# Linear attention: the last sum of a tile moved from VectorE to a ScalarE copy and a GpSimd sum

## The chip, the core and the metric

The kernel runs on one core of a Trainium2 chip. The metric is the device time of one execution in microseconds (us). The engines are TensorE (PE, with its weight loads as PEld), VectorE (DVE), ScalarE (ACT), GpSimd (POOL) and SyncE (SP). Each works through its own queue in order, and the order between engines is made by waits on semaphores.

## What is computed

The input x has 2048 rows of 128 floats. Four blocks follow each other, each on the layer norm of x and added back to x: softmax attention (16 heads of 64), a mixture of experts (8 experts, one chosen per row), a linear attention (16 heads of 8), and the same mixture of experts again. The change is in the linear attention:

```python
qkv = x @ w_qkv.T + b_qkv
q, k, v = jnp.split(qkv, 3, axis=-1)        # 16 heads of 8
q_prime = elu(q) + 1.0
k_prime = elu(k) + 1.0
kv_cumsum = cumsum(einsum('bhtd,bhte->bhtde', k_prime, v), axis=2)
context = einsum('bhtd,bhtde->bhte', q_prime, kv_cumsum)
norm = einsum('bhtd,bhtd->bht', q_prime, cumsum(k_prime, axis=2))
out = context / (norm[..., None] + EPS)
return out @ w_out.T + b_out                # added to x
```

## The kernel before

The four blocks are `attention`, `ffn`, `linear_attention` and `ffn`, with a barrier of all engines behind each. `linear_attention` (L1318) handles 16 tiles of 128 rows. Every engine runs the same software pipeline, `in_turn` (L1374): turn n emits, for each stage with offset off, the work on tile n - off, in the order in which the stages stand in that engine's dictionary. The offsets and that order are written out by hand, engine by engine; there is no planner. Buffers come in pairs (tile t uses number t % 2), and waits on counters keep a buffer from being overwritten.

The path of tile t:

- norm, GpSimd, turn t (L1393): xn is x less its mean, times 1/deviation, with statistics from VectorE made ahead of the pipeline.
- xT, turn t: TensorE transposes (L1575), ScalarE copies to SBUF (L1492).
- z, turn t + 1: TensorE projects to q, k, v (L1581); ScalarE makes neg, v and ex (L1504 to L1507). features on VectorE (L1446) make qk of them.
- turn t + 2: TensorE transposes q (L1548, copied by ScalarE at L1482), GpSimd makes outer, the products of k and v with 1152 columns (L1413), TensorE adds to past (L1554, L1556; ScalarE copies it, L1487), then makes the prefix sums within the tile as a matmul of outer with a triangle (L1564), and inter, the part of earlier tiles (L1571). VectorE multiplies the sums with q (prod, L1439).
- heads, VectorE, turn t + 3: reduce (L1449), add inter (L1453), den (L1457, L1459), and o (L1463). GpSimd masks past into state (L1402), read by inter of tile t + 1.
- turn t + 4: TensorE transposes o (L1585), ScalarE copies it (oT, L1512). GpSimd adds the output bias into x (bias, L1397).
- y, turn t + 5: TensorE projects oT into `out` in PSUM (L1544), one bank, not a pair; VectorE adds `out` to x (L1435). TensorE's y of the next tile waits for that sum (s_x).

The orders, with offsets: GpSimd norm 0, outer 2, state 3, bias 4. VectorE heads 3, features 1, y 5, sums 2. ScalarE qT 2, z 1, xT 0, past 2, oT 4. TensorE qT 2, z 1, y 5, xT 0, sums 2, oT 4. The second and third transposes share a PSUM bank with the first, so TensorE's qT of a turn waits for ScalarE's oT copy of the turn before (L1525). The last tile's work ends in turn 20.

Of the kernel before, what the change touches and what calls it, by code (L numbers as in the profile page):

```python
# [10 lines left out]
ALU = mybir.AluOpType  # L11
ACT = mybir.ActivationFunctionType
AX = mybir.AxisListType

P = 128
# [1302 lines left out]
def linear_attention(nc, shp, keep):  # L1318

    D, NT = shp.D, shp.NT  # L1320
# [3 lines left out]
    U = 2  # L1324
    x, ident = keep["x"], keep["ident"]
# [4 lines left out]
    with ExitStack() as ctx:  # L1330
        def sb(name, shape, dt=F32):
            return ctx.enter_context(nc.sbuf_tensor("li_" + name, shape, dt))

        def pair(name, shape):
            return [sb(f"{name}{k}", shape) for k in range(U)]
# [3 lines left out]
        def sem(name):  # L1339
            sems.append(nc.alloc_semaphore("li_" + name))  # L1340
            return sems[-1]

        def psum(name, cols):
# [5 lines left out]
        past, inter, out = past_ps[:, 0:VX], inter_ps[:, 0:VX], out_ps[:, 0:D]  # L1349
# [3 lines left out]
        xn, xT = pair("xn", [P, D]), pair("xT", [D, P])  # L1353
        neg, ex = pair("neg", [P, 2 * D]), pair("ex", [P, 2 * D])
        qk, v1 = pair("qk", [P, 2 * D]), pair("v1", [P, HL, DL + 1])

        outer, prod = pair("outer", [P, HL, DL + 1, DL]), sb("prod", [P, HL, DL + 1, DL])
        qT, mine, state = pair("qT", [D, P]), pair("mine", [P, VX]), pair("state", [P, VX])
        own, tot = sb("own", [P, HL, DL + 1]), sb("tot", [P, HL, DL + 1])
        den, o, oT = sb("den", [P, HL]), pair("o", [P, HL, DL]), pair("oT", [P, P])  # L1360

        s_one, s_xb, s_den = sem("s_one"), sem("s_xb"), sem("s_den")
# [1 line left out]
        s_xn, s_xTp, s_xT, s_z, s_neg, s_ex, s_v, s_qk = (sem(n) for n in ("s_xn", "s_xTp", "s_xT", "s_z", "s_neg", "s_ex", "s_v", "s_qk"))  # L1364
        s_outer, s_sums, s_prod, s_past, s_mine, s_state, s_inter = (
            sem(n) for n in ("s_outer", "s_sums", "s_prod", "s_past", "s_mine", "s_state", "s_inter"))
        s_qTp, s_qT, s_own, s_tot, s_rden, s_o, s_oTp, s_oT, s_out, s_x = (
            sem(n) for n in ("s_qTp", "s_qT", "s_own", "s_tot", "s_rden", "s_o", "s_oTp", "s_oT", "s_out", "s_x"))

        def rows_of(c):  # L1370

            return slice(0, TPC) if c == 0 else slice(TPC, NT)

        def in_turn(offsets, emit):  # L1374
            for n in range(NT + max(offsets.values())):
                for stage, off in offsets.items():
                    if 0 <= n - off < NT:
                        emit(stage, n - off, (n - off) % U)

        with nc.Block() as block:  # L1380

            @block.gpsimd
            def _(pool):
                for k in range(U):
                    pool.memset(v1[k][:, :, DL:DL + 1], 1.0).then_inc(s_one, 1)
                pool.wait_ge(li["s_bo"], 16)

                def emit(stage, t, k):
                    if stage == "norm":
                        pool.wait_ge(s_rstd, 1 if t < TPC else 2)  # L1390
                        if t >= U:
                            pool.wait_ge(s_xTp, t - U + 1)
                        pool.tensor_scalar(xn[k][:, :], x[:, t, :], mv[:, t, 0:1], rstd[:, t:t + 1],  # L1393
                                           ALU.subtract, ALU.mult).then_inc(s_xn, 1)
                    elif stage == "bias":
                        pool.wait_ge(s_xn, t + 1)
                        pool.tensor_tensor(x[:, t, :], x[:, t, :], b_out_all[:, :], ALU.add).then_inc(s_xb, 1)  # L1397
                    elif stage == "state":
                        pool.wait_ge(s_mine, t + 1)
                        if t >= U:  # L1400
                            pool.wait_ge(s_inter, t - 1)
                        pool.tensor_tensor(state[k][:, :], mine[k][:, :], block_mask[:, :, :].rearrange("p h e -> p (h e)"),  # L1402
                                           ALU.mult).then_inc(s_state, 1)
                    else:
                        pool.wait_ge(s_qk, t + 1)
                        pool.wait_ge(s_v, t + 1)
                        if t == 0:
                            pool.wait_ge(s_one, U)
                        if t >= U:
                            pool.wait_ge(s_sums, t - U + 1)  # L1410
                        kk = qk[k][:, D:2 * D].rearrange("p (h d) -> p h d", d=DL).unsqueeze(2).to_broadcast([P, HL, DL + 1, DL])
                        vv = v1[k][:, :, :].unsqueeze(3).to_broadcast([P, HL, DL + 1, DL])
                        pool.tensor_tensor(outer[k][:, :, :, :], kk, vv, ALU.mult).then_inc(s_outer, 1)  # L1413

                in_turn({"norm": 0, "outer": 2, "state": 3, "bias": 4}, emit)

            @block.vector
            def _(dve):
                for c in range(2):
                    tiles = range(NT)[rows_of(c)]  # L1420
                    for t in tiles:
                        if t % TPC == 0:
                            dve.wait_ge(keep["s_x"][t // TPC], 16)
                        dve.bn_stats(stats[:, t, :], x[:, t, :]).then_inc(s_stat, 1)
                    for t in tiles:
                        dve.wait_ge(s_stat, t + 1)
                        dve.bn_aggr(mv[:, t, :], stats[:, t, :]).then_inc(s_aggr, 1)
                    dve.wait_ge(s_std, c + 1)
                    dve.reciprocal(rstd[:, rows_of(c)], rstd[:, rows_of(c)]).then_inc(s_rstd, 1)

                def emit(stage, t, k):
                    if stage == "y":
                        dve.wait_ge(s_out, t + 1)
                        dve.wait_ge(s_xb, t + 1)
                        dve.tensor_tensor(x[:, t, :], out, x[:, t, :], ALU.add).then_inc(s_x, 1)  # L1435
                    elif stage == "sums":
                        dve.wait_ge(s_sums, t + 1)
                        qq = qk[k][:, 0:D].rearrange("p (h d) -> p h d", d=DL).unsqueeze(2).to_broadcast([P, HL, DL + 1, DL])
                        dve.tensor_tensor(prod[:, :, :, :], sums_ps[:, 0:OUTER].rearrange("p (h e d) -> p h e d", e=DL + 1, d=DL),  # L1439
                                          qq, ALU.mult).then_inc(s_prod, 1)  # L1440
                    elif stage == "features":
                        dve.wait_ge(s_ex, t + 1)
                        if t >= U:
                            dve.wait_ge(s_qTp, t - U + 1)
                            dve.wait_ge(s_past, t - U + 1)
                        dve.scalar_tensor_tensor(qk[k][:, :], z_ps[:, 0:2 * D], 0.0, ex[k][:, :], ALU.max, ALU.add).then_inc(s_qk, 1)  # L1446
                    else:
                        dve.wait_ge(s_prod, t + 1)
                        dve.tensor_reduce(own[:, :, :], prod[:, :, :, :], AX.X, ALU.add).then_inc(s_own, 1)  # L1449
                        dve.wait_ge(s_own, t + 1)  # L1450
                        if t:
                            dve.wait_ge(s_inter, t)
                            dve.tensor_tensor(tot[:, :, :], inter.rearrange("p (h e) -> p h e", e=DL + 1), own[:, :, :], ALU.add).then_inc(s_tot, 1)  # L1453
                        else:
                            dve.tensor_copy(tot[:, :, :], own[:, :, :]).then_inc(s_tot, 1)
                        dve.wait_ge(s_tot, t + 1)
                        dve.tensor_scalar(den[:, :].unsqueeze(2), tot[:, :, DL:DL + 1], EPS, None, ALU.add).then_inc(s_den, 1)  # L1457
                        dve.wait_ge(s_den, t + 1)
                        dve.reciprocal(den[:, :], den[:, :]).then_inc(s_rden, 1)  # L1459
                        dve.wait_ge(s_rden, t + 1)  # L1460
                        if t >= U:
                            dve.wait_ge(s_oTp, t - U + 1)
                        dve.tensor_tensor(o[k][:, :, :], tot[:, :, 0:DL], den[:, :].unsqueeze(2).to_broadcast([P, HL, DL]), ALU.mult).then_inc(s_o, 1)  # L1463

                in_turn({"heads": 3, "features": 1, "y": 5, "sums": 2}, emit)

            @block.scalar
            def _(act):
# [6 lines left out]
                deviation(0)  # L1475

                def emit(stage, t, k):
                    if stage == "qT":
                        act.wait_ge(s_qTp, t + 1)
                        if t > U:  # L1480
                            act.wait_ge(s_inter, t - U)
# [29 lines left out]
                            act.wait_ge(s_out, t - U + 1)  # L1511
                        act.activation(oT[k][:, :], oT_ps, ACT.Copy).then_inc(s_oT, 1)  # L1512

                in_turn({"qT": 2, "z": 1, "xT": 0, "past": 2, "oT": 4}, emit)

            @block.tensor
            def _(pe):
# [21 lines left out]
                def emit(stage, t, k):  # L1539
                    if stage == "y":  # L1540
                        pe.wait_ge(s_oT, t + 1)
                        if t:
                            pe.wait_ge(s_x, t)
                        pe.matmul(out, oT[k][:, :], wT[:, 3, :], start=True, stop=True).then_inc(s_out, 1)  # L1544
                    elif stage == "qT":
                        pe.wait_ge(s_qk, t + 1)
# [169 lines left out]
```

## Time and profile before

| what | us |
|---|---|
| median of 3 runs | 1243.08 (1242.02 to 1244.05) |
| the profiled execution, its own time | 1235.74 |
| its span | 1234.0 |
| busy: TensorE, VectorE, GpSimd, ScalarE | 1135.5, 930.9, 832.8, 808.1 |
| linear attention in the trace | about 1056 to 1141 |
| its steady part, turns 5 to 15 | 1078 to 1124 |

The trace gives the start and duration of each instruction from the start of the span. In square brackets stands how long the engine had been idle before it, and what it waited for last. `PE L1564 x6` is six matmuls merged into one row. "issue" is idle time with no wait that the profile shows. Ends of matmuls are modelled, and spans on GpSimd are rough.

### The profile page before, as it was taken

What the parts mean: (1) busy time and instruction counts of PE and PEld (TensorE: products, weight loads), DVE (VectorE), ACT (ScalarE), POOL (GpSimd) and SP (SyncE); (2) the same over time, 40 slices, a digit from 0 to 9 for tenths busy, and PEclk for the clock granted to TensorE, in tenths of its full rate; (3) what the DMA queues carried; (4) which work ended last, traced back from release to release, by engine and by line L of the source; (5) the groups of instructions that cost most, each with busy time, mean ns of one, the idle gap of its engine ahead of it and who ended that gap; (6) DMA issues with size and microseconds to landing.
All of it is one profiled execution on the core that took longest, in us unless ns stands there. A gap on an engine that the chain in (4) does not pass through costs nothing. (4 is left out here: it accounts for less than half of the span.)

```text
span 1234.0 us, 24704 instructions
## 1 busy us (share of the span) xinstructions
PE 1135.5 (92%) x8010; PEld 847.9 (69%) x8010; DVE 930.9 (75%) x2054; ACT 808.1 (65%) x2248; POOL 832.8 (67%) x814
## 2 busy tenths in 40 slices
PE   6999999999999999999999999999999669687477
PEld 4776677677767776777677767767776559354377
DVE  5887878787787778778877787788787546598645
ACT  6877676767786767777777767776777346342355
POOL 3687678857786788677677757785878435585434
PEclk9999999999999999999999999999999879799579
DMA  5000810081018002700450063002004232100131
GB/s 145 27 1 1 210 49 2 6 229 35 1 35 224 2 1 58 209 1 2 117 141 1 2 176 92 1 18 52 2 1 126 86 92 67 35 1 1 56 98 50
DMA packets 72908, 75.71 MB, mean 61 GB/s; under 512 B 8487, under 2 KB 61869, under 8 KB 72784
## 3 DMA queue, kind: packets, MB, share of 16 engines
q1 hardware_dynamic: 69776, 67.80, 20.6%
q0 software_dynamic: 3008, 6.34, 1.5%
q8 instruction: 68, 1.11, 0.4%
q14 instruction: 56, 0.46, 0.1%
HBM read 15.34 MB, written 42.91 MB: 47 GB/s over the span
## 5 line engine op out<-in xcount | busy, mean ns | idle before, releaser
L604 DVE TENSOR_REDUCE at_nmax<-at_ps 128x1 f32<-128x512 f32 (+3 forms) x640 | 374.6, 603 | 122.0 <-PE at_ps L853 119.1
L510 POOL TENSOR_SCALAR at_prob<-at_prob,at_scale 128x512 f32<-128x512 f32 (+3 forms) x307 | 424.5, 1401 | 2.0
L850 PE MATMUL at_ps<-at_k_st,at_q_parts 128*128 128x512 f32 (+3 forms) x640 | 285.6, 446 | 4.0 <-DVE at_q_parts L663 2.0
L721 ACT ACTIVATE at_prob<-at_ps,at_nmax 128x512 f32<-128x512 f32 (+3 forms) x416 | 259.9, 631 | 43.5 <-DVE at_nmax L604 42.7
L879 PE MATMUL at_ps<-at_probT,at_v 128*64 128x256 f32 (+1 forms) x2304 | 270.1, 374 | 0.6 <-DVE at_probT L627 0.6
L734 ACT ACTIVATE at_probT<-at_ps 128x512 f32<-128x512 f32 (+1 forms) x288 | 165.2, 574 | 148.8 <-PE at_ps L864 122.6
L853 PE MATMUL at_ps<-at_k_st,at_q_parts 128*128 128x512 f32 (+3 forms) x640 | 252.2, 394 | 0.0
L627 DVE COPY at_probT<-at_ps 128x512 f32<-128x512 f32 (+1 forms) x288 | 189.1, 657 | 51.6 <-PE at_ps L864 42.8
L510 POOL TENSOR_SCALAR late<-late,at_scale 128x512 f32<-128x512 f32 (+1 forms) x168 | 226.4, 1364 | 1.6
L864 PE MATMUL at_ps<-ident,at_prob 128*128 128x128 f32 x1440 | 220.1, 273 | 5.1 <-DVE at_probT L627 4.3
L879 PEld LDWEIGHTS at_ps<-at_probT,at_v 128*64 128x64 f32 x2304 | 152.1, 136 | 102.5 <-issue 40.9
L864 PEld LDWEIGHTS at_ps<-ident,at_prob 128*128 128x128 f32 x1440 | 172.8, 140 | 57.4 <-issue 23.7
L721 ACT ACTIVATE late<-at_ps,at_nmax 128x512 f32<-128x512 f32 (+1 forms) x224 | 135.4, 611 | 29.9 <-DVE at_nmax L604 27.2
L850 PEld LDWEIGHTS at_ps<-at_k_st,at_q_parts 128*128 128x128 f32 x640 | 121.0, 189 | 47.3 <-issue 27.9
L853 PEld LDWEIGHTS at_ps<-at_k_st,at_q_parts 128*128 128x128 f32 x640 | 124.8, 195 | 0.8 <-issue 0.5
L864 PE MATMUL at_ps<-ident,late 128*128 128x128 f32 x736 | 109.9, 273 | 0.0
L864 PEld LDWEIGHTS at_ps<-ident,late 128*128 128x128 f32 x736 | 89.4, 140 | 19.0 <-issue 3.1
L489 POOL TENSOR_TENSOR at_gap<-at_low,at_nmax 128x8 f32<-128x8 f32 (+2 forms) x48 | 10.1, 210 | 132.1 <-DVE at_low L609 132.1
L721 ACT ACTIVATION_READ_ACCUMULATOR at_prob<-at_ps,at_nmax 128x1 f32 x416 | 85.4, 205 | 0.0
L897 PE MATMUL at_ps<-late 128*128 128x512 f32 x128 | 69.7, 628 | 2.8 <-DVE at_q_parts L663 1.1
L1171 ACT ACTIVATE f_hT<-f_ps,f_wfix 128x128 f32<-128x128 f32 x184 | 52.7, 371 | 24.8 <-issue 18.8
L634 DVE TENSOR_SCALAR at_prob<-at_prob,at_scale 128x512 f32<-128x512 f32 (+1 forms) x104 | 64.1, 627 | 1.7 <-POOL at_scale L504 0.7
(241 smaller groups left out, 1488.3 us busy)
## 6 DMA issues: line engine op xcount, KB each, us to landing
slots_in<-empty SPq DMA_DIRECT2D x6, 2967.0 KB, 18.9
slots_in<-empty SPq DMA_DIRECT2D x6, 2838.0 KB, 18.4
at_q_parts<-at_q_parts SPq DMA_DIRECT2D x64, 256.0 KB, 3.5
f_xs<-slots_in SPq DMA_DIRECT2D x46, 129.0 KB
late<-in_L_ffn_w_dram SPq DMA_DIRECT2D x1, 2048.0 KB, 9.0
late<-in_L_ffn_w_dram SPq DMA_DIRECT2D x4, 512.0 KB, 6.6
rows<-in_L_attn_a_x_dram SPq DMA_DIRECT2D x4, 256.0 KB, 3.8
rows<-new_x SPq DMA_DIRECT2D x4, 256.0 KB, 3.7
```

The costliest lines, as they stand in the source:

```text
L510: pool.tensor_scalar(cols, cols, scale[:, k, u, c:c + 1], None, ALU.mult).then_inc(s_fix["pool"], 1)
L604: dve.tensor_reduce(nmax[:, q % 2, 2 * i + h, c:c + 1], bank, AX.X, ALU.max, negate=True).then_inc(s_max, 1)
L627: dve.tensor_copy(probT[1][n % TURNED][:, 0:w], turn_ps[1][:, 0:w]).then_inc(s_probT[1], 1)
L634: dve.tensor_scalar(cols, cols, scale[:, k, u, c:c + 1], None, ALU.mult).then_inc(s_fix["dve"], 1)
L721: act.activation(prob[ROW_HOME[j]][u][:, c * BANK:c * BANK + w], ring[use_of["score", p, j, i, h, c] % RING][:, 0:w], ACT.Exp, bias=nmax[: ...
L734: act.activation(probT[0][n % TURNED][:, 0:w], turn_ps[0][:, 0:w], ACT.Copy).then_inc(s_probT[0], 1)
L850: pe.matmul(bank[:, 0:w], q_hi[h][:, r * P:(r + 1) * P], keys, start=True, stop=False)
L853: pe.matmul(bank[:, 0:w], q_lo[h][:, r * P:(r + 1) * P], keys, start=False, stop=True).then_inc(s_score, 1)
L864: last = pe.transpose(turn_ps[h][:, b * P:(b + 1) * P], prob[ROW_HOME[j]][2 * i + h][:, t * P:(t + 1) * P], ident[:, :])
L879: last = pe.matmul(z_ps[part_of, to:to + w], v[:, t, part_of], probT[h][group[p, j, g] % TURNED][:, 2 * P * b:2 * P * b + w], start=t == 0 ...
L897: pe.matmul(ring[use_of[it] % RING][:, :], wT["kq"[i]][:, p, :], xnT[:, c * BANK:(c + 1) * BANK], start=True, stop=True).then_inc(s_proj, 1)
L1171: last = act.activation(hT[k][:, f, :], ps[2 + s % 2][:, f * P:(f + 1) * P], ACT.Gelu, bias=wfix[k][:, B1.start + f:B1.start + f + 1])
```

## The change

ScalarE copies the projected rows from PSUM to a new pair of SBUF buffers `y`, and GpSimd adds that buffer to x. The stage y (offset 5) leaves VectorE's order. In ScalarE's it stands between xT and past, in GpSimd's between outer and state. TensorE's next projection waits for ScalarE's copy (s_y) instead of the sum (s_x). The values computed are the same.

```diff
+        y = pair("y", [P, D])
...
@@ gpsimd
+                    elif stage == "y":
+                        pool.wait_ge(s_xb, t + 1)
+                        pool.wait_ge(s_y, t + 1)
+                        pool.tensor_tensor(x[:, t, :], y[k][:, :], x[:, t, :], ALU.add).then_inc(s_x, 1)
...
-                in_turn({"norm": 0, "outer": 2, "state": 3, "bias": 4}, emit)
+                in_turn({"norm": 0, "outer": 2, "y": 5, "state": 3, "bias": 4}, emit)
@@ vector
-                    if stage == "y":
-                        dve.wait_ge(s_out, t + 1)
-                        dve.wait_ge(s_xb, t + 1)
-                        dve.tensor_tensor(x[:, t, :], out, x[:, t, :], ALU.add).then_inc(s_x, 1)
-                    elif stage == "sums":
+                    if stage == "sums":
...
-                in_turn({"heads": 3, "features": 1, "y": 5, "sums": 2}, emit)
+                in_turn({"heads": 3, "features": 1, "sums": 2}, emit)
@@ scalar
+                    if stage == "y":
+                        act.wait_ge(s_out, t + 1)
+                        if t >= U:
+                            act.wait_ge(s_x, t - U + 1)
+                        act.activation(y[k][:, :], out, ACT.Copy).then_inc(s_y, 1)
...
-                in_turn({"qT": 2, "z": 1, "xT": 0, "past": 2, "oT": 4}, emit)
+                in_turn({"qT": 2, "z": 1, "xT": 0, "y": 5, "past": 2, "oT": 4}, emit)
@@ tensor
                     if stage == "y":
                         pe.wait_ge(s_oT, t + 1)
                         if t:
-                            pe.wait_ge(s_x, t)
+                            pe.wait_ge(s_y, t)
```

## Rows read from the trace of the kernel before

**Rows 1.** Stretches: busy time per engine (instructions), granted clock, DMA share; steady part

```profile
1085.00:1127.00 42.00, 37.41 (x174) 24.36 (x173) 39.15 (x73) 16.94 (x64) 34.14 (x36) 1.00 0.00 1
```

**Rows 2.** Order of time, one turn, TensorE (start us, us, engine, line)

```profile
1090.98 0.38 PE L1544 MATMUL li_outp<-li_wT,li_oT 128*128 128x128 f32 x2
...
1091.80 2.10 PE L1564 MATMUL li_sums<-li_outer,li_upto 128*128 128x512 f32 x6
...
1093.74 0.41 PE L1571 MATMUL li_interp<-li_state,li_qT 128*128 128x144 f32 x2
...
1093.99 0.27 PE L1585 MATMUL li_turnp<-ident,li_o 128*128 128x128 f32 x1
...
1094.72 0.30 PE L1548 MATMUL li_turnp<-ident,li_qk 128*128 128x128 f32 x1 [0.46 <-ACT li_oT L1512]
```

**Rows 3.** Order of time, the same turn, ScalarE

```profile
1091.92 0.37 ACT L1492 ACTIVATE li_xT<-li_turnp,ones 128x128 f32<-128x128 f32 x1
...
1092.17 0.30 ACT L1487 ACTIVATE li_mine<-li_pastp 128x144 f32<-128x144 f32 x1
...
1094.30 0.28 ACT L1512 ACTIVATE li_oT<-li_turnp 128x128 f32<-128x128 f32 x1 [1.82 <-PE li_turnp L1585]
```

**Rows 4.** Order of time, the same turn, GpSimd

```profile
1089.10 2.17 POOL L1413 TENSOR_TENSOR li_outer<-li_qk,li_v 128x1152 f32<-128x1152 f32 x1 [0.77 <-DVE li_qk L1446]
...
1091.23 0.49 POOL L1402 TENSOR_TENSOR li_state<-li_mine,li_block_mask 128x144 f32<-128x144 f32 x1
...
1091.68 0.41 POOL L1397 TENSOR_TENSOR rows<-rows,li_b_out_all 128x128 f32<-128x128 f32 x1
...
1092.07 0.80 POOL L1393 TENSOR_SCALAR li_xn<-rows,li_mv,li_rstd 128x128 f32<-128x128 f32 x1
...
1093.68 2.17 POOL L1413 TENSOR_TENSOR li_outer<-li_qk,li_v 128x1152 f32<-128x1152 f32 x1 [0.81 <-DVE li_qk L1446]
```

**Rows 5.** Order of time, the same turn, VectorE

```profile
1092.97 0.29 DVE L1463 TENSOR_TENSOR li_o<-li_tot,li_den 128x128 f32<-128x128 f32 x1
...
1093.18 0.41 DVE L1446 SCALAR_TENSOR_TENSOR li_qk<-li_zp,li_ex 128x256 f32<-128x256 f32 x1
...
1093.52 0.28 DVE L1435 TENSOR_TENSOR rows<-li_outp,rows 128x128 f32<-128x128 f32 x1
...
1093.94 1.36 DVE L1439 TENSOR_TENSOR li_prod<-li_sums,li_qk 128x1152 f32<-128x1152 f32 x1
```

**Rows 6.** Order of time, outer of turn 4, the sums of turns 4, 5, 15

```profile
1071.13 2.18 POOL L1413 TENSOR_TENSOR li_outer<-li_qk,li_v 128x1152 f32<-128x1152 f32 x1 [2.76 <-DVE li_qk L1446]
...
1073.36 2.21 PE L1564 MATMUL li_sums<-li_outer,li_upto 128*128 128x512 f32 x6 [0.62 <-POOL li_outer L1413]
...
1078.05 2.10 PE L1564 MATMUL li_sums<-li_outer,li_upto 128*128 128x512 f32 x6
...
1123.89 2.10 PE L1564 MATMUL li_sums<-li_outer,li_upto 128*128 128x512 f32 x6
```

**Rows 7.** Order of time, the drain of the stage

```profile
1138.49 0.29 DVE L1463 TENSOR_TENSOR li_o<-li_tot,li_den 128x128 f32<-128x128 f32 x1
...
1139.13 0.46 PE L1544 MATMUL li_outp<-li_wT,li_oT 128*128 128x128 f32 x2 [3.03 <-DVE rows L1435]
...
1139.43 0.27 PE L1585 MATMUL li_turnp<-ident,li_o 128*128 128x128 f32 x1
...
1140.65 0.29 DVE L1435 TENSOR_TENSOR rows<-li_outp,rows 128x128 f32<-128x128 f32 x1 [0.73 <-PE li_outp L1544]
```

**Rows 8.** Order of time, VectorE's o beside GpSimd, late and early

```profile
1133.79 0.83 POOL L1397 TENSOR_TENSOR rows<-rows,li_b_out_all 128x128 f32<-128x128 f32 x2
...
1134.19 0.58 DVE L1463 TENSOR_TENSOR li_o<-li_tot,li_den 128x128 f32<-128x128 f32 x1
...
1074.11 0.82 POOL L1393 TENSOR_SCALAR li_xn<-rows,li_mv,li_rstd 128x128 f32<-128x128 f32 x1
...
1074.57 0.29 DVE L1463 TENSOR_TENSOR li_o<-li_tot,li_den 128x128 f32<-128x128 f32 x1
```

More of the change, by code:

```diff
@@ L1366, in linear_attention @@
             sem(n) for n in ("s_outer", "s_sums", "s_prod", "s_past", "s_mine", "s_state", "s_inter"))
-        s_qTp, s_qT, s_own, s_tot, s_rden, s_o, s_oTp, s_oT, s_out, s_x = (
-            sem(n) for n in ("s_qTp", "s_qT", "s_own", "s_tot", "s_rden", "s_o", "s_oTp", "s_oT", "s_out", "s_x"))
+        s_qTp, s_qT, s_own, s_tot, s_rden, s_o, s_oTp, s_oT, s_out, s_x, s_y = (
+            sem(n) for n in ("s_qTp", "s_qT", "s_own", "s_tot", "s_rden", "s_o", "s_oTp", "s_oT", "s_out", "s_x", "s_y"))
         def rows_of(c):
@@ L1477, in emit @@
                 def emit(stage, t, k):
-                    if stage == "qT":
+                    if stage == "y":
[3 more added lines that the diff above has]
+                        act.activation(y[k][:, :], out, ACT.Copy).then_inc(s_y, 1)
+                    elif stage == "qT":
                         act.wait_ge(s_qTp, t + 1)
```

## The prediction

> **What bounds the stage now.** I read the stretches first, because only the linear attention (about 1056 to 1141 us) is touched. In its steady part TensorE's clock is granted in full and VectorE, TensorE and GpSimd are busy 39.2, 37.4 and 34.1 us of 42 [rows 1]. Busy shares name three suspects, so I went to the order of time of one turn, engine by engine. A turn n is one pass of `in_turn`: tile n is normalised in it, tile n-5 gets its final sum.
>
> TensorE comes first [rows 2]. From the output projection (1090.98) through the prefix sums (1091.80), inter (1093.74) and the transpose of o (1093.99) it has no gap; then it idles 0.46 us until ScalarE has copied oT, and starts the next turn (1094.72). The prefix sums start at 1078.05 in turn 5 and at 1123.89 in turn 15 [rows 6]: 45.84 us, so a turn is 4.584 us. All of it is TensorE's own work plus that round trip to ScalarE, so TensorE bounds the loop. VectorE has almost no slack [rows 5]: y ends at 1093.80, the product starts at 1093.94, once the sums are there. GpSimd idles 0.81 us before outer, until qk is made [rows 4].
>
> Below, A is the time at which TensorE gets to the prefix sums of a turn (1091.80 here), S when it starts them (now S = A). Outer of turn n must be finished by then: it ends at 1089.10 + 2.17 = A - 0.53. That half microsecond is the cover which the change spends.
>
> **Removed.** On VectorE 16 sums of 0.28 us [rows 5]. Without them VectorE goes from qk straight to the product; qk starts 0.76 us ahead of it, and the product waits for TensorE's sums anyhow. In the steady part I cost this at nothing: TensorE's turn hides it.
>
> **Added on ScalarE.** A copy of 128x128 out of PSUM, 0.28 us like the oT copy [rows 3]. It stands behind z and xT in ScalarE's order. xT starts at A + 0.12 and the next instruction 0.25 later, so the copy of y starts at A + 0.37 and ends at A + 0.65. Queued behind it is the copy of past (0.30 us), which then comes about 0.2 us later; its readers are GpSimd's state and TensorE's past, both a turn later, over 3 us away. ScalarE has 1.8 us idle before oT [rows 3], so it isn't delayed. TensorE's y now waits for the copy of the tile before, made a turn ago: nothing.
>
> **Added on GpSimd, and this is the cost.** The sum costs what the bias sum of the same shape does, 0.41 to 0.45 us [rows 4]. 0.81 us were idle, so by busy time it fits. But it stands right behind outer, and waits for the copy of the same turn. Outer ends at A - 0.53; the copy is there at A + 0.65. GpSimd stands still for over a microsecond, and behind it in its queue are state, bias, and the norm of the next tile, and then the next outer, on which TensorE depends.
>
> Step by step: GpSimd starts after ScalarE as it does after VectorE (qk ends 1093.18 + 0.41 = 1093.59, outer starts 1093.68: 0.09), so y starts at A + 0.74. From start to start: y to state 0.42 (bias to norm is 0.39 to 0.44), state to bias 0.45, bias to norm 0.41, norm to outer 0.77 (0.80, less the overlap of the others) [rows 4]. The next outer starts at A + 2.79, not A + 1.88, and ends at A + 4.96. TensorE starts 0.05 to 0.06 after it, as in turn 4 (outer 1071.13 + 2.18, sums 1073.36) [rows 6]. So the next S is not earlier than A + 5.02, against 4.584 until now. A turn that began with such a wait also lasts longer, from S to the next A: 1078.05 - 1073.36 = 4.69, not 4.584, since the weights are not loaded ahead [rows 6].
>
> Now the two loops together. From turn 5, S = A = 0. A(6) = 4.584; S(6) = 5.02, a wait of 0.44. A(7) = 5.02 + 4.69 = 9.71; the outer asks for A(6) + 5.02 = 9.60, so no wait in turn 7. So the wait comes every second turn: two turns last 9.71 instead of 9.17, **+0.54 a pair**. The delayed turns are 6 to 15 (the first y is in turn 5; from turn 16 no norm stands between y and outer, and the 0.77 us it frees covers the rest): 5 pairs, **+2.7 us**. The state product in GpSimd's turn now ends at about A + 1.65; inter reads it at A + 1.94 [rows 2]: covered, by 0.2 us.
>
> **The drain.** Today TensorE's y of tile 14 (1139.13) waits 3.03 us for VectorE's sum of tile 13, which is queued behind the last heads; the last transpose of o comes behind it at 1139.43, although o ended at 1138.49 + 0.29 = 1138.78 [rows 7]. With ScalarE releasing the bank it can start 0.06 after o's end (the step from outer to the sums in turn 4), at 1138.84: -0.59. Behind the last projection stood 0.04 + 0.29 us of VectorE (to 1140.94); now 0.04 + 0.28 (ScalarE) + 0.09 + 0.43 (GpSimd) = 0.84: +0.51. Net -0.1.
>
> **VectorE against GpSimd.** In the last turns o took 0.58 us where it takes 0.29, started together with a sum on GpSimd; but at 1074.57 it took 0.29 within a norm of GpSimd [rows 8]. Today o (1092.97) starts just after the norm ends (1092.87) [rows 4, 5]; after the change it falls, at A + 1.1 to A + 1.2, on state and bias. The Trainium skill (SBUF — State Buffer, Who interferes with whom) says that a VectorE instruction with two SBUF inputs and a GpSimd one that reads SBUF exclude each other for the whole instruction. By that rule, GpSimd's sum beside the long o agrees; the norm beside the short one does not. If VectorE only waits, its 0.29 us are hidden, since GpSimd now is later than qk by some 0.9 us; only in turn 16, without a norm, qk of tile 15 is on the path; there bias, started up to 0.2 after o would, could hold o for up to 0.4, so 0 to 0.4, and I take 0.2. If GpSimd waits, up to 0.29 a turn lengthens its chain, half of which shows in the turn: 0 to +1.5 us. I take 0, since the two sums beside the long o took 0.83 us, their usual time [rows 8]. The skill's GPSIMD Engine Reference (Engine selection) also calls a two-input operation about twice as slow there as on VectorE; an estimate by it is 0.56 us for the sum and some 0.6 us more in total. The bias rows, at 0.41 to 0.45 us, say that 0.28 us on VectorE becomes 0.43 here.
>
> **Sum.** 2.7 - 0.1 + 0.2 = +2.8 us. The profiled execution took 1235.74, 7.3 us under the median of the three timed runs; it would become 1238.6. On the median of 1243.08: 1245.9.
>
> Bounds: ScalarE to GpSimd as fast as TensorE to ScalarE, 0.04: -0.3; weights loaded ahead after all: -0.5; so +2.0. ScalarE's xT at its full 0.37 before the copy: +0.6; GpSimd's steps each at full duration: +0.6; exclusion on GpSimd's side: +1.5; so +5.5.
>
> **Rivals.**
> (a) The exclusion hits GpSimd in every turn: 2.8 + 1.5, 1247.4. For it: o moves into GpSimd's busy part. Against: no lengthened instruction of GpSimd [rows 8]. It is the case that the Trainium skill's rule on the shared port would make, had VectorE the first claim.
> (b) The wait is mostly hidden: GpSimd's 0.81 us idle takes the 0.43 us up, as busy time suggests, and the drain gives the rest: 1243.0 to 1244.5. It needs the copy some 0.9 us earlier than ScalarE's order gives it; a shorter chain by 0.44 us would do. Against: the steps above.
> (c) Faster: VectorE, not TensorE, bounds the loop. It decides where qk follows late enough that the product starts behind y rather than behind the sums; then each of some 11 turns saves the 0.34 us from qk to y: -3.7, 1239.3. For it: only 0.14 us between y and product, and qk gates outer too. Against: TensorE is gapless up to its wait for ScalarE [rows 2].
> (d) TensorE idles more (now 0.46, then some 0.7 us a turn) and its clock falls to the lower of its two levels for a stretch, here or into the next stage: +3 to +10 us more. The rows show 1.00 beside 11% idle [rows 1].
>
> **Chances.** Forecast 0.50, (a) 0.15, (b) 0.23, (c) 0.06, (d) 0.06. A measurement of this kernel can tell about 0.2%, 2.5 us. The forecast's own 2.0 to 3.8 straddles that bound; I count seven tenths of it above. Slower: 0.35 + 0.15 + 0.06 = 0.56. Same: 0.15 + 0.23 = 0.38. Faster 0.06. The range 1243.4 to 1248.6 holds the forecast, (a), half of (b) and the upper bounds.
>
> **What would show it.** Right: outer's idle time put down no longer to qk, and y on GpSimd idle over a microsecond before each start, ended by ScalarE's copy; the prefix sums waiting 0.4 us for outer in every second turn; starts of the sums in turns 5 and 15 apart by 48.5 us; the last transpose of o 0.6 us sooner after o's end. Wrong: TensorE's only wait still oT, the distance still 45.8 (b), or below (c); GpSimd's state or bias longer than 0.6 us (a); a granted clock below 1 in the loop (d).

## The result and the profile after

| | before | after |
|---|---|---|
| median, us | 1243.70 (13 runs, 1242.02 to 1244.57) | 1246.70 (13 runs, 1245.70 to 1247.85) |
| ratio, 95% interval | | 1.0028 (1.0020 to 1.0036) |
| start of the prefix sums, turn 5 to turn 15, us | 45.84 | 49.09 |
| the same, turn 15 to the end of the last sum with y, us | 17.05 | 17.85 |

The medians are 3.0 us apart (0.24%); the ratio and its interval say 3.5 us (2.5 to 4.5). Either way the change is a small loss. The third row of the table will serve for every run below: it is ten turns of the loop, read from one profile, and it repeats far better than the total does. In five of the variants the stretch came out within 0.01 us of before's 45.84, while the medians can tell about 1 us at best.

Busy time per engine in the steady part, which answers to [rows 1], and in the drain (the last turns, in which the pipeline runs empty):

```profile
1082.00:1131.00 49.00, 43.39 (x193) 27.43 (x192) 42.53 (x71) 20.26 (x83) 42.31 (x50) 1.00 0.00 1
...
1146.00:1150.00 4.00, 1.27 (x3) 0.69 (x3) 0.56 (x3) 0.55 (x2) 0.84 (x2) 0.50 0.00 0
```

GpSimd is now busy 42.3 of 49 us (it was 34.1 of 42), VectorE 42.5, TensorE 43.4. TensorE did the same work and is idle 5.6 us of 49, where it was 4.6 of 42; its sums take 2.21 instead of 2.10 us when they had to wait, and count as busy. The granted clock is 1.00 through the loop; from 1146 it is at 0.50, the lower level, in the drain, where TensorE had waited 1.89 us for the last o. Now who waited for whom between 1080 and 1130 (total us, times, longest):

```profile
POOL rows L1402 <- ACT li_y L1483: 7.0, 10, 1.4
...
PE li_turnp L1554 <- ACT li_oT L1518: 5.0, 11, 0.5
DVE li_prod L1440 <- PE li_sums L1570: 4.9, 8, 0.9
...
PE li_sums L1570 <- POOL li_outer L1418: 0.8, 3, 0.3
...
POOL li_outer L1418 <- DVE li_qk L1447: 0.4, 1, 0.4
```

The first row did not exist before: GpSimd stands still before its sum until ScalarE's copy is there. Outer's wait for qk, which came to 9.9 us in as long a stretch before, is 0.4. TensorE's wait for ScalarE's oT is unchanged, and it has a second one, on outer. The 0.8 us listed there are not the whole loss of 3.25: the ends of matmuls are modelled, and most of the later waits vanish behind the matmuls ahead of them (TensorE's "busy" time grows from 4.08 to 4.35 us a turn for the same work). VectorE, which lost the sum, waits 4.9 us for TensorE's sums. One pair of turns in order of time (turns 5 and 6, all engines; answers to [rows 2 to 5]):

```profile
1082.29 2.10 PE L1570 MATMUL li_sums<-li_outer,li_upto 128*128 128x512 f32 x6
1082.41 0.37 ACT L1498 ACTIVATE li_xT<-li_turnp,ones 128x128 f32<-128x128 f32 x1
...
1082.66 0.29 ACT L1483 ACTIVATE li_y<-li_outp 128x128 f32<-128x128 f32 x1
...
1083.09 0.41 POOL L1402 TENSOR_TENSOR rows<-li_y,rows 128x128 f32<-128x128 f32 x1 [1.39 <-ACT li_y L1483]
...
1083.46 0.49 POOL L1407 TENSOR_TENSOR li_state<-li_mine,li_block_mask 128x144 f32<-128x144 f32 x1
1083.46 0.63 DVE L1464 TENSOR_TENSOR li_o<-li_tot,li_den 128x128 f32<-128x128 f32 x1
...
1083.90 0.51 POOL L1398 TENSOR_TENSOR rows<-rows,li_b_out_all 128x128 f32<-128x128 f32 x1
...
1084.40 0.79 POOL L1394 TENSOR_SCALAR li_xn<-rows,li_mv,li_rstd 128x128 f32<-128x128 f32 x1
...
1085.16 2.17 POOL L1418 TENSOR_TENSOR li_outer<-li_qk,li_v 128x1152 f32<-128x1152 f32 x1
...
1087.38 2.21 PE L1570 MATMUL li_sums<-li_outer,li_upto 128*128 128x512 f32 x6 [0.34 <-POOL li_outer L1418]
...
1088.05 0.29 DVE L1464 TENSOR_TENSOR li_o<-li_tot,li_den 128x128 f32<-128x128 f32 x1
1088.09 0.60 POOL L1407 TENSOR_TENSOR li_state<-li_mine,li_block_mask 128x144 f32<-128x144 f32 x1
...
1092.07 2.16 PE L1570 MATMUL li_sums<-li_outer,li_upto 128*128 128x512 f32 x6
```

The chain goes as it was drawn: sums at A = 1082.29, xT, copy of y at A + 0.37, GpSimd's sum at A + 0.80, then state, bias, norm, outer, and TensorE starts the next sums at A + 5.09, after a wait of 0.34 us. Turn 6 lasts 4.69 us. (A is the time at which TensorE gets to the prefix sums of a turn.) New are the long instructions: o takes 0.63 us in turn 5; in turn 6 o takes 0.29 but state 0.60 instead of 0.49. The drain, which answers to [rows 7]:

```profile
1146.33 0.29 DVE L1464 TENSOR_TENSOR li_o<-li_tot,li_den 128x128 f32<-128x128 f32 x1
...
1146.68 0.48 PE L1591 MATMUL li_turnp<-ident,li_o 128*128 128x128 f32 x1 [1.89 <-DVE li_o L1464]
...
1147.52 0.80 PE L1550 MATMUL li_outp<-li_wT,li_oT 128*128 128x128 f32 x2 [0.37 <-ACT li_oT L1518]
1148.36 0.28 ACT L1483 ACTIVATE li_y<-li_outp 128x128 f32<-128x128 f32 x1 [0.88 <-PE li_outp L1550]
1148.78 0.45 POOL L1402 TENSOR_TENSOR rows<-li_y,rows 128x128 f32<-128x128 f32 x1 [2.38 <-ACT li_y L1483]
```

The last transpose of o starts 0.35 us after o does; before it was 0.94. The chain behind it is longer, and its matmuls take 0.48 and 0.80 us, on the lower clock level, where they took 0.27 and 0.55.

### The profile page after: what moved, and what is told of

The parts are those of the page before. It is cut to its first block and busy times, and to the rows that moved or that the text cites. A ratio compares the mean times of both kernels' runs of the same rounds, so it can differ in the third digit from the quotient of the medians.

```text
span 1244.0 us, 24734 instructions
## 1 busy us (share of the span) xinstructions
PE 1138.5 (92%) x8010; PEld 849.1 (68%) x8010; DVE 930.3 (75%) x2038; ACT 810.0 (65%) x2264; POOL 839.7 (67%) x830
## 5 line engine op out<-in xcount | busy, mean ns | idle before, releaser
L627 DVE COPY at_probT<-at_ps 128x512 f32<-128x512 f32 (+1 forms) x288 | 189.3, 657 | 52.2 <-PE at_ps L864 43.4
```

What stands on the lines that cost most here:

```text
L627: dve.tensor_copy(probT[1][n % TURNED][:, 0:w], turn_ps[1][:, 0:w]).then_inc(s_probT[1], 1)
```

## Experiments

In each, "loop" is the stretch from turn 5 to turn 15, read from one profile. Each ratio is against the kernel before, run beside the variant on the same chip (medians 1238.1 to 1243.5 us), and comes from 11 or 12 runs of the variant, from 5 for e7 and e12. The names in the text are the first parts of the labels.

| run | what it isolates | loop, us | ratio to before (95%) |
|---|---|---|---|
| before | | 45.84 | |
| the change | | 49.09 | 1.0028 (1.0020 to 1.0036) |
| e1_sum_last | GpSimd's sum behind state and bias | 45.85 | 1.0001 (0.9992 to 1.0010) |
| e2_sum_turn_later | GpSimd's sum a turn later | 45.85 | 0.9997 (0.9988 to 1.0005) |
| e3_copy_earlier | ScalarE's copy earlier | 45.84 | 1.0005 (0.9997 to 1.0014) |
| e4_work_without_wait | work alone | 45.85 | 0.9998 (0.9989 to 1.0006) |
| e5_wait_without_work | wait alone | 47.17 | 1.0013 (1.0002 to 1.0024) |
| e6_scalar_part_alone | ScalarE's copy, VectorE's sum | 45.85 | 0.9998 (0.9989 to 1.0007) |
| e7_tot_in_psum | o with one operand from SBUF | 48.63 | 1.0035 (1.0022 to 1.0048) |
| e8_before_z_first | before, TensorE's wait filled | 44.76 | 1.0001 (0.9992 to 1.0010) |
| e9_after_z_first | e2, the same edit | 44.95 | 1.0003 (0.9993 to 1.0013) |
| e10_before_past_ahead | e8, past ahead of xT | 45.03 | 0.9998 (0.9987 to 1.0009) |
| e11_after_past_ahead | e9, past ahead of xT | 44.74 | 1.0004 (0.9993 to 1.0015) |
| e12_qk_before_heads | e11, qk ahead of the heads | 58.80 | 1.0162 (1.0145 to 1.0178) |

**Place, work or wait.** The theory was that GpSimd's sum stands still for a copy that comes late in the same turn, and that what is queued behind it pays. The rivals: the 0.43 us of work on a slower engine, or the copy on ScalarE. Moving the sum behind state and bias, e1:

```diff
-                in_turn({"norm": 0, "outer": 2, "y": 5, "state": 3, "bias": 4}, emit)
+                in_turn({"norm": 0, "outer": 2, "state": 3, "bias": 4, "y": 5}, emit)
```

> The change, with y moved behind state and bias in GpSimd's order; the same work and the same wait. Measures: the time against before, and the distance between the starts of the prefix sums of turns 5 and 15 (before 45.84 us, after the change 49.09 us). Theory (what stands behind the waiting sum in GpSimd's queue is the cost): state and bias now run while GpSimd would wait, outer starts near A + 2.0 and ends before TensorE needs it: distance 45.8 to 46.0 us, time 0 to +0.8 us against before. Rival (the 0.43 us of work on GpSimd is the cost): distance near 49, time +3 us. Rival (the copy on ScalarE delays past and xT): as after the change, +3 us.

```profile
1093.79 0.49 POOL L1407 TENSOR_TENSOR li_state<-li_mine,li_block_mask 128x144 f32<-128x144 f32 x1
...
1094.15 2.10 PE L1570 MATMUL li_sums<-li_outer,li_upto 128*128 128x512 f32 x6
1094.24 0.42 POOL L1398 TENSOR_TENSOR rows<-rows,li_b_out_all 128x128 f32<-128x128 f32 x1
...
1094.95 0.45 POOL L1402 TENSOR_TENSOR rows<-li_y,rows 128x128 f32<-128x128 f32 x1 [0.29 <-ACT li_y L1483]
...
1096.25 2.17 POOL L1418 TENSOR_TENSOR li_outer<-li_qk,li_v 128x1152 f32<-128x1152 f32 x1
...
1098.73 1.45 PE L1570 MATMUL li_sums<-li_outer,li_upto 128*128 128x512 f32 x3
```

State and bias fill most of the wait (0.29 us is left of it), outer starts at A + 2.10, and TensorE never notices: 4.58 us to the next sums. (Where a row of sums counts fewer than six matmuls, the view ended inside them.) The loss is gone, though GpSimd does the same sum and needs the same copy; only its place in the queue differs. So is it when the sum is taken up a turn later, e2:

```diff
-                in_turn({"norm": 0, "outer": 2, "y": 5, "state": 3, "bias": 4}, emit)
+                in_turn({"norm": 0, "y": 6, "outer": 2, "state": 3, "bias": 4}, emit)
```

> The change, with GpSimd's sum a turn later (offset 6) and ahead of outer, so that its wait has long been met; the same work. Theory: distance 45.8 us, outer waits for qk again (some 0.35 us of idle), time 0 to +0.8 us against before. Rival (work on GpSimd): distance near 49, +3 us. Rival (VectorE and GpSimd exclude each other): some 0.1 us a turn stays even so, but is hidden, distance 45.8.

The loop is 45.85, and outer waits for qk again, 0.56 us in two turns of three. And with GpSimd's order left as in the change, but the copy made sooner, e3:

```diff
-                in_turn({"qT": 2, "z": 1, "xT": 0, "y": 5, "past": 2, "oT": 4}, emit)
+                in_turn({"qT": 2, "y": 5, "z": 1, "xT": 0, "past": 2, "oT": 4}, emit)
```

> The change, with only ScalarE's order altered: y ahead of z and xT. GpSimd's order is that of the change. Theory (the lateness of the copy against outer's end decides): the copy ends near A - 0.1, GpSimd's sum starts near A + 0.0, outer near A + 2.1; distance 45.8 to 46.2 us, time 0 to +0.8 us against before, although z's and xT's copies come 0.3 to 0.4 us later. Rival (work on GpSimd): +3 us. Rival (ScalarE is the tight engine): distance over 49, since z comes later.

```profile
1094.97 0.28 ACT L1483 ACTIVATE li_y<-li_outp 128x128 f32<-128x128 f32 x1 [0.65 <-PE li_outp L1550]
...
1095.37 2.10 PE L1570 MATMUL li_sums<-li_outer,li_upto 128*128 128x512 f32 x6
1095.39 0.45 POOL L1402 TENSOR_TENSOR rows<-li_y,rows 128x128 f32<-128x128 f32 x1 [0.27 <-ACT li_y L1483]
...
1097.52 2.17 POOL L1418 TENSOR_TENSOR li_outer<-li_qk,li_v 128x1152 f32<-128x1152 f32 x1
...
1099.95 1.45 PE L1570 MATMUL li_sums<-li_outer,li_upto 128*128 128x512 f32 x3
```

The copy starts 0.40 us ahead of A instead of 0.37 behind it, GpSimd's sum at A + 0.02, and the loop is before's, although GpSimd still waits 0.27 us in every turn. All three came out as the theory had it. The pieces alone, put into the kernel before. Work, e4:

```diff
+                    elif stage == "extra":
+                        pool.tensor_tensor(spare[:, t, :], b_out_all[:, :], b_out_all[:, :], ALU.add)
...
-                in_turn({"norm": 0, "outer": 2, "state": 3, "bias": 4}, emit)
+                in_turn({"norm": 0, "outer": 2, "extra": 5, "state": 3, "bias": 4}, emit)
```

> The kernel before, with an extra sum of 128x128 on GpSimd in the place that the change uses, with no wait and into a spare buffer; VectorE still makes the real sum. Theory: hidden in GpSimd's 0.81 us of idle time, distance 45.84 us, time within 0.3 us of before. Rival (work on GpSimd is the cost): distance up to 49, time +2 to +3 us.

Nothing, as expected: the extra sum of 0.40 us took outer's wait for qk from about 0.8 to 0.44 us. Wait, e5 (the copy is made, GpSimd waits for it where the change's sum stands, VectorE sums):

```diff
+                    elif stage == "hold":
+                        pool.wait_ge(s_y, t + 1)
...
-                in_turn({"norm": 0, "outer": 2, "state": 3, "bias": 4}, emit)
+                in_turn({"norm": 0, "outer": 2, "hold": 5, "state": 3, "bias": 4}, emit)
```

> The kernel before, with ScalarE's copy of y made as well, and GpSimd only waiting for it in the place that the change uses, with no sum; VectorE still makes the real sum (after the copy). Theory (wait and work add up in one chain: wait to A + 0.8, then state, bias, norm, outer): outer starts near A + 2.45, the prefix sums may start near A + 4.67 where TensorE comes at A + 4.58 to 4.69; distance 46.3 to 46.9 us, time +0.5 to +1.2 us against before. Rival (the wait alone is the whole cost): distance near 49. Rival (the wait costs nothing, only work does): 45.84.

```profile
1090.17 2.10 PE L1572 MATMUL li_sums<-li_outer,li_upto 128*128 128x512 f32 x6
...
1090.90 0.49 POOL L1405 TENSOR_TENSOR li_state<-li_mine,li_block_mask 128x144 f32<-128x144 f32 x1 [0.93 <-ACT li_y L1484]
...
1091.35 0.60 POOL L1398 TENSOR_TENSOR rows<-rows,li_b_out_all 128x128 f32<-128x128 f32 x1
...
1092.70 2.17 POOL L1416 TENSOR_TENSOR li_outer<-li_qk,li_v 128x1152 f32<-128x1152 f32 x1
...
1094.92 0.30 PEld L1572 LDWEIGHTS li_sums<-li_outer,li_upto 128*128 128x128 f32 x2 [0.22 <-POOL li_outer L1416]
```

The wait alone costs 1.33 us of the loop, more than the 0.5 to 1.1 that the expected stretch allowed. The rows show the missing part: bias takes 0.60 us beside o, which starts in the same moment (both at 1091.35), so the sums start 4.75 us after the last ones and not 4.67. So wait and work don't each have a price: work alone costs 0, the wait alone 1.3, both in one queue 3.25, because they lie in one chain of which the first part was covered. ScalarE's half alone, e6:

```diff
-                in_turn({"norm": 0, "outer": 2, "y": 5, "state": 3, "bias": 4}, emit)
+                in_turn({"norm": 0, "outer": 2, "state": 3, "bias": 4}, emit)
@@ vector
+                    if stage == "y":
+                        dve.wait_ge(s_y, t + 1)
+                        dve.wait_ge(s_xb, t + 1)
+                        dve.tensor_tensor(x[:, t, :], y[k][:, :], x[:, t, :], ALU.add).then_inc(s_x, 1)
```

> The change with its GpSimd half undone: ScalarE copies y to SBUF, TensorE's next projection waits for the copy, and VectorE sums from SBUF in its old place. Theory: distance 45.84 us; the drain gives some 0.3 us back (the projection of tile 14 no longer waits behind VectorE's heads), time -0.5 to +0.2 us against before. Rival (the copy on ScalarE is what costs): distance near 49, +3 us. VectorE's sum now has two SBUF inputs; if it and outer exclude each other, outer starts up to 0.2 us later in each turn, hidden.

The loop is 45.85, and turn 15 to the last sum took 16.77 us (1126.61 to 1143.38), 0.28 less than before: the drain's gain, once the last sum is VectorE's. In the median it can't be told from 0.

**The long o.** In the change's rows o takes 0.63 us in one turn and state 0.60 in the next. The theory is that o on VectorE, with both operands in SBUF, and an instruction of GpSimd that reads SBUF hold each other up (the exclusion). e7 keeps tot in PSUM, so that o reads one operand from SBUF:

```diff
-        own, tot = sb("own", [P, HL, DL + 1]), sb("tot", [P, HL, DL + 1])
+        own, tot = sb("own", [P, HL, DL + 1]), inter_ps[:, VX:2 * VX].rearrange("p (h e) -> p h e", e=DL + 1)
...
-                            if t >= 2:
-                                pe.wait_ge(s_tot, t)
+                            pe.wait_ge(s_o, t)
```

> The change, with tot held in spare columns of inter's PSUM bank, so that VectorE's o reads only one operand from SBUF; TensorE's inter waits for o instead of tot. Theory (exclusion between o and GpSimd's state and bias lengthens GpSimd's chain by 0.05 to 0.1 us a turn): o takes about 0.3 us in every turn, not 0.63 in every second one; state stays at 0.49, not 0.60; distance 48.4 to 48.8 us against 49.09. Rival (the lengthened rows have another cause): they stay, distance 49.1.

```profile
1094.97 2.21 PE L1570 MATMUL li_sums<-li_outer,li_upto 128*128 128x512 f32 x6 [0.29 <-POOL li_outer L1418]
...
1095.32 0.45 POOL L1402 TENSOR_TENSOR rows<-li_y,rows 128x128 f32<-128x128 f32 x1 [0.40 <-ACT li_y L1483]
...
1095.70 0.29 DVE L1464 TENSOR_TENSOR li_o<-li_interp,li_den 128x128 f32<-128x128 f32 x1
1095.73 0.49 POOL L1407 TENSOR_TENSOR li_state<-li_mine,li_block_mask 128x144 f32<-128x144 f32 x1
...
1100.83 0.49 POOL L1407 TENSOR_TENSOR li_state<-li_mine,li_block_mask 128x144 f32<-128x144 f32 x1
1100.84 0.29 DVE L1464 TENSOR_TENSOR li_o<-li_interp,li_den 128x128 f32<-128x128 f32 x1
```

In the same places and beside the same instructions o takes 0.29 us in every turn and state 0.49. The loop falls from 49.09 to 48.63. So 0.46 us of it, some 0.05 a turn, was the exclusion between o and GpSimd. The edit also lets den read tot from PSUM and makes inter wait for o; den takes 0.17 us in the loop of both kernels. The run's own time (1.0035, five runs) does not resolve the 0.46 us.

**Could the removed sum pay?** If TensorE's wait for oT is what bounds the loop before, filling it should make VectorE the bound, and then its lighter load should show. e8, on the kernel before, and e9, on e2:

```diff
-                in_turn({"qT": 2, "z": 1, "y": 5, "xT": 0, "sums": 2, "oT": 4}, emit)
+                in_turn({"z": 1, "qT": 2, "y": 5, "xT": 0, "sums": 2, "oT": 4}, emit)
```

> The kernel before, with TensorE's z ahead of qT in its turn, so that the projection fills TensorE's 0.46 us wait for the copy of oT. Theory: TensorE's turn shrinks to some 4.2 to 4.3 us and VectorE, with y in its order, becomes the bound at 4.44 us (4.584 less its 0.14 of idle time); distance 44.2 to 44.8 us, time -1.2 to -2.2 us against before. Rival (TensorE still waits for ScalarE, now ahead of xT): 45.84.

> The change with GpSimd's sum a turn later and ahead of outer (as in the run of that kind), and TensorE's z ahead of qT. Theory: the removed sum on VectorE now pays, since VectorE is the bound once TensorE's wait is filled: VectorE needs 4.16 us, TensorE 4.2 to 4.3, GpSimd 4.2; distance 42 to 43.5 us, time -2.5 to -4 us against before, 1 to 2 us better than the kernel before with z first. Rival (the sum on VectorE never mattered): no better than that kernel.

e8's loop fell by 1.08 us, within what was expected, though the ratio doesn't show it. From turn 5 to the end of the last sum only 0.34 us of it is left (62.55 against 62.89): the last turns, some of whose matmuls were on the lower clock level, give the rest back. e9 missed: 44.95, no better than e8. In the waits of e9 TensorE stands 1.9 us in ten turns, ahead of xT, for ScalarE's copy of qT. Taking that out too, e10 on e8 and e11 on e9:

```diff
-                in_turn({"z": 1, "qT": 2, "y": 5, "xT": 0, "sums": 2, "oT": 4}, emit)
+                in_turn({"z": 1, "qT": 2, "y": 5, "past": 2, "xT": 0, "sums": 2, "oT": 4}, emit)
```

> The kernel before, with TensorE's z first and its two matmuls of past ahead of xT, so that xT no longer waits 0.17 us for ScalarE's copy of qT. VectorE still makes the sum. Theory: VectorE bounds the loop at 4.48 us, as with z first alone, where it never waited; distance 44.6 to 44.9 us, time 0 to -1.5 us against before. Rival (TensorE's stall bounded that kernel): distance under 44.

> The change with GpSimd's sum a turn later and ahead of outer, TensorE's z first and past ahead of xT. Theory: with the sum off VectorE and TensorE's 0.17 us stall gone, the turn is bounded by TensorE at 4.2 to 4.4 us or by GpSimd, which has 4.2 to 4.3 us of work; distance 42.5 to 44 us, 1 to 2 us less than the same order with the sum on VectorE, time -1.5 to -3 us against before. Rival (VectorE's sum pays nowhere): distance as in the same order with the sum on VectorE.

e10 came out at 45.03, just over the expected stretch, and e11 missed again, with 44.74. Its trace shows why:

```profile
1093.52 2.21 PE L1571 MATMUL li_sums<-li_outer,li_upto 128*128 128x512 f32 x6 [0.39 <-POOL li_outer L1418]
...
1095.76 1.36 DVE L1440 TENSOR_TENSOR li_prod<-li_sums,li_qk 128x1152 f32<-128x1152 f32 x1 [0.34 <-PE li_sums L1571]
...
1099.75 0.41 DVE L1447 SCALAR_TENSOR_TENSOR li_qk<-li_zp,li_ex 128x256 f32<-128x256 f32 x1
...
1100.24 2.17 POOL L1418 TENSOR_TENSOR li_outer<-li_qk,li_v 128x1152 f32<-128x1152 f32 x1 [0.56 <-PE li_interp L1578]
...
1102.47 0.70 PE L1571 MATMUL li_sums<-li_outer,li_upto 128*128 128x512 f32 x1 [0.39 <-POOL li_outer L1418]
```

Sums to product 2.24 us, product to qk 3.99, qk to outer 0.49, outer to the next-but-one sums 2.23: 8.95 us for two turns, and the starts of the sums are 1093.52 and 1102.47. Each step starts as soon as the one before it allows: VectorE has no gap between product and qk (o takes 0.45 us there instead of 0.29, beside GpSimd's sum), and outer starts 0.08 us after qk's end (its row names inter, for which outer does not wait in the kernel). The loop over three engines closes without the sum with y, which stood behind qk in VectorE's order. In the kernel before [rows 5, 6, with qk one turn of 4.584 us on] the same sum is 2.14 + 3.83 + 0.50 + 2.22 = 8.69 us, against 9.17 for two turns of TensorE: a TensorE without stalls could win no more than 0.24 us a turn.

VectorE's sum lies in neither of these two bounds, but it does lie in a third, VectorE's own queue. In the kernel before, that queue has 0.14 us to spare in each turn [rows 5]. In e8 and e10 it has none from 1084 us on, with the sum between qk and product (e10):

```profile
1102.01 0.42 DVE L1446 SCALAR_TENSOR_TENSOR li_qk<-li_zp,li_ex 128x256 f32<-128x256 f32 x1
...
1102.35 0.28 DVE L1435 TENSOR_TENSOR rows<-li_outp,rows 128x128 f32<-128x128 f32 x1
...
1102.54 1.35 DVE L1439 TENSOR_TENSOR li_prod<-li_sums,li_qk 128x1152 f32<-128x1152 f32 x1
```

So once TensorE's wait is filled, VectorE bounds the kernel with the sum, at 4.50 us a turn in e10, as expected. Without it (e11) VectorE waits again, 0.34 us before every second product, and the loop over three engines holds the turn at 4.47. What the removed sum gives back is the distance between these two, 0.03 us a turn. That the three-engine loop is the bound is read off the traces; no run shortened it cleanly. The last run takes it on: qk right behind the reduce.

```diff
-                in_turn({"heads": 3, "features": 1, "sums": 2}, emit)
+                in_turn({"own": 3, "features": 1, "heads": 3, "sums": 2}, emit)
```

> The run before it (the change with the sum a turn later, z first, past ahead of xT), with one more edit: VectorE makes qk right after the reduce, ahead of tot, den and o. Theory: what bounded the last runs is a loop over three engines and two turns, sums 2.24, product to qk 3.99, outer 2.25, which add up to the 8.95 us measured for two turns and in which the final sum does not stand. qk comes 1.0 to 1.2 us sooner, so the loop falls under 8 us for two turns and TensorE or GpSimd bounds at 4.2 to 4.4 us; distance 42.5 to 44 us, time -1.5 to -3.5 us against before. Rival (each engine's own work bounds the turn at 4.47 already): distance 44.5 to 45.

It missed widely: 5.88 us a turn.

```profile
1102.10 0.41 DVE L1447 SCALAR_TENSOR_TENSOR li_qk<-li_zp,li_ex 128x256 f32<-128x256 f32 x1
...
1102.59 2.17 POOL L1418 TENSOR_TENSOR li_outer<-li_qk,li_v 128x1152 f32<-128x1152 f32 x1 [1.60 <-DVE li_qk L1447]
...
1102.76 2.03 DVE L1459 TENSOR_SCALAR li_den<-li_tot 128x16 f32<-128x16 f32 x1
...
1105.33 1.35 DVE L1440 TENSOR_TENSOR li_prod<-li_sums,li_qk 128x1152 f32<-128x1152 f32 x1
...
1106.82 1.96 PE L1572 MATMUL li_sums<-li_outer,li_upto 128*128 128x512 f32 x4 [1.70 <-DVE li_prod L1440]
```

With qk early, outer starts early, and den, which reads and writes 16 columns in SBUF and took 0.17 us, now starts inside outer and takes 2.03: it ends at 1104.79, just after outer at 1104.76. Product and the next sums come behind it, and VectorE has no gap in the 5.88 us. Whether the shorter loop would otherwise have paid stays open; no run had den free of outer, and that was not tried.

No version beats the kernel before in its measured time. e8 to e11 have loops about 1 us shorter, of which 0.3 to 0.4 us is left by the end of the last sum, and intervals of 0.1% can't confirm that.

## Why the prediction was right

Predicted 1245.9 on a median of 1243.08, a difference of +2.8; measured +3.0 by the medians, +3.5 by the ratio (2.5 to 4.5). The mechanism was right. That 2.8 and 3.0 lie so close is partly luck: the traces give 3.25 us in the loop and 0.3 in the drain, some 3.6 in all, and the prediction was low in both. By its steps:

- **TensorE bounds the loop, VectorE's sum is free.** Shown: with the sum off VectorE and no other loss (e1, e2, e3) the loop is before's to 0.01 us; and with TensorE's wait filled (e8) it gets shorter. What was not seen is how close the next bounds lie: VectorE's own queue at 4.44 us a turn (4.584 less 0.14), and the loop over three engines at 8.69 us for two.
- **ScalarE's copy is free.** Shown by e6, which keeps the copy and leaves the sum on VectorE.
- **The cost is the wait in GpSimd's queue, not the work alone.** Shown from five sides (e1 to e5). Rival (b), that busy time decides, falls for the change as made, but it is what happens as soon as the sum stands elsewhere (e1, e2).
- **+2.7 us in the loop.** The steps gave 5.02 and 4.69 us for a pair of turns; the first pair took 5.09 and 4.69. ScalarE to GpSimd is 0.14 us, not 0.09, and the exclusion came on top. Later the wait spreads over both turns of a pair instead of every second (5.09 and 4.69 at first, 4.93 and 4.91 at the end), with the sum nearly the same. Total 3.25. Without the exclusion, e7, it is 2.79.
- **The exclusion on GpSimd's side, taken as 0 within 0 to 1.5.** It was 0.46: rival (a) is real at a third of its price. The row on which the 0 rested [rows 8] showed only the order in which GpSimd's instruction was first. Where o is first, state takes 0.60; and where GpSimd is first, the instruction behind it, bias, takes 0.51. With norm it is alike: where o starts up to 0.07 us ahead of norm (e1, e3), norm takes 0.89 to 0.94 us instead of 0.79, and where norm is 0.46 us or more ahead, o keeps its 0.29 ([rows 8], and every turn of e4's loop). The rule of the Trainium skill (SBUF — State Buffer, Who interferes with whom), that the one which starts first keeps the port for its whole instruction, agrees with den behind outer (0.17 us became 2.03). It is too strict for the small ones: state loses only 0.11 us to an o that runs on for 0.25, and a norm already running does not hold o.
- **The drain, -0.1, and +0.2 for turn 16.** The drain's two parts and turn 16 were right in sign, the net too low. The transpose came 0.59 us sooner after o, as predicted. The end of the chain behind the last projection is 0.91 instead of 0.33 us, +0.58 against +0.51 predicted. Turn 16, at 4.58, cost 0.10, since its weights had not been loaded ahead, and turn 17 another 0.18, where den took 0.35 instead of 0.17 beside a sum of GpSimd and made qk late; the prediction had put it down to a long o, which kept its 0.29. In the profiled execution some 0.46 more is the lower clock level in the last matmuls. e1, with 0.33 and 0.49 us for them, did not have it, and e4 and e8, which lack GpSimd's sum, have it too (0.79 us for the last projection), so I don't count it as the change's. Without it the drain costs 0.3.
- **Clock, rival (d).** Not in the loop: granted 1.00. In this stage the lower level stands only in the drain, as above.
- **The signs.** Outer's wait for qk is gone, ScalarE's copy ends GpSimd's wait, the transpose is 0.6 us sooner, the distance is 49.09 for 48.5. One sign did not come as written: GpSimd was to idle over a microsecond before each sum, and did so once in the loop (1.39 us in turn 5, then 0.35 to 0.90), since the loss itself makes outer late and shortens the next wait for the copy.

The profiled executions differ by 10.3 us (1235.74 and 1246.02), their spans by 10.0. Of that, 4.2 us is there before the first sum with y is made (the sums of turn 4 start at 1073.36 and 1077.60), so it isn't the change's. From there to the last sum with y it is 4.05, and 1.7 lies behind the stage, in code that is the same and whose length differs by up to 4.4 us between the traces of all runs (93.05 to 97.42). The medians, not the two profiles' spans, carry the result.

## What to carry to other kernels

An instruction moved to an engine with idle time is cheap only if its operand is there when its turn comes: in a queue worked in order, ask first when the operand arrives against when the queue gets there, and put the instruction behind what is ready, or a turn later. Here the same work on the same engine cost 3 us in one place and nothing in two others. Before work is taken off a busy engine, follow the loop that sets the turn all the way round, over engines and turns; if the work isn't on it, nothing comes back, however busy the engine looks. And if it is on it, what comes back ends at the next bound, here 0.03 us a turn away.

## What the hardware showed beyond what was expected

- VectorE's `tensor_scalar` of 128x16 in SBUF, 0.17 us, took 2.03 us when it started 0.17 us behind the start of a GpSimd `tensor_tensor` of 2.17 us, in every turn of e12's loop. The loop grew from 44.74 us (e11) to 58.80.
- The exclusion works both ways and is small for small instructions: o 0.29 to 0.63 us, state 0.49 to 0.60, bias 0.41 to 0.51 (0.60 in e5), norm 0.79 to 0.94 (e1).
- A GpSimd instruction that waits for ScalarE starts 0.14 us after it (copy 1082.66 + 0.29, sum 1083.09); one that waits for VectorE, 0.09 [rows 4, 5].
